# A graph network's first sum takes its first eight source tiles by halves of 256 columns, from block 6 on, then two tiles a block

## What is computed

```
h = relu(layernorm(x)); h = relu(h @ enc_w1.T + enc_b1) @ enc_w2.T + enc_b2
for w in conv_w:                                  # 5 layers
    agg = segment_sum((h @ w)[src], dst)          # sum over a node's edges
    gi, gh = agg @ gru_wih.T + gru_bih, h @ gru_whh.T + gru_bhh
    r = sigmoid(ir + hr); z = sigmoid(iz + hz); n = tanh(i_n + r * h_n)
    h = (1 - z) * n + z * h
x = x + sigmoid(relu(relu(h) @ dec_w1.T + dec_b1) @ dec_w2.T + dec_b2)
h = relu(layernorm(x))
out = x + (A @ relu((A @ h) @ W1.T + b1)) @ W2.T + b2   # A: normalized adjacency
```

## Time and profile before

| | us |
|---|---|
| median of three runs (lowest, highest) | 739.68 (739.09, 739.78) |
| the profiled execution | 739.29 |
| its span | 737.4 |
| PE busy | 720.2 (98%) |
| DVE busy | 331.2 (45%) |
| ACT busy | 316.5 (43%) |

### The profile page before, as it was taken

The page is one execution under the profiler, slowest core; times in us unless marked ns, Lnnn a source line. Parts: engine busy times, 40 slices in busy tenths (PEclk is TensorE's granted clock), DMA queues, the critical chain, the costliest instruction groups (busy, mean ns, idle before and its releaser), DMA issues.

```text
span 737.4 us, 9911 instructions
## 1 busy us (share of the span) xinstructions
PE 720.2 (98%) x4071; PEld 394.2 (53%) x4071; DVE 331.2 (45%) x665; ACT 316.5 (43%) x467; POOL 43.6 (6%) x57
## 2 busy tenths in 40 slices
PE   6989999999999999999999999999999999999998
PEld 4556666445444454444444444444445545558887
DVE  7999997625032241133221223656644632122532
ACT  5978876737244344244452334432447411122000
POOL 4230000000000000000000000120002220000000
DMA  6020000835003232022230212610002000000100
GB/s 168 4 91 10 3 4 3 157 60 90 2 6 64 55 53 39 1 49 44 59 64 0 49 37 38 119 61 2 1 0 93 15 1 1 1 1 3 37 24 32
DMA packets 79240, 28.41 MB, mean 39 GB/s; under 512 B 70519, under 2 KB 78390, under 8 KB 79062
## 3 DMA queue, kind: packets, MB, share of 16 engines
q1 hardware_dynamic: 78230, 26.93, 17.1%
q0 software_dynamic: 240, 0.66, 0.3%
q10 hardware_dynamic: 720, 0.13, 0.1%
HBM read 8.03 MB, written 2.60 MB: 14 GB/s over the span
## 4 chain that ended last, share of the span: by engine, by line
PE 85%; DVE 9%; ACT 2%; DMA 1%; POOL 1%; issue 1%; SPq 0%; ACTq 0%; DVEq 0%; POOLq 0%
PE PSA L1260 35%; PE PSA L1477 9%; PE PSA L1342 7%; PE PSA L1421 5%; PE PSA L1205 4%; PE PSA L1273 4%; PE PSA L1282 4%; PE PSA L1281 3%; PE PSA L1277 3%; PE PSA L1275 3%; PE PSA L1284 3%; DVE CT L877 3%; PE PSA L1409 2%; PE PSA L1397 1%; DVE stat L839 1%; DMA H<-yS 1%
## 5 line engine op out<-in xcount | busy, mean ns | idle before, releaser
L1260 PE MATMUL PSA<-AT,H 128*128 128x512 fp8e3 (+1 forms) x1470 | 275.8, 347 | 0.3 <-DMA H<-yS 0.2
L1260 PEld LDWEIGHTS PSA<-AT,H 128*128 128x128 f16 x1470 | 126.7, 98 | 151.4 <-issue 12.0
L1090 DVE SCALAR_TENSOR_TENSOR rS<-PSA,bias,rS 128x512 f32<-128x512 f32 (+1 forms) x35 | 23.9, 683 | 261.0 <-ACT rS L1660 261.0
L1660 ACT ACTIVATE rS<-PSA,bias 128x512 f32<-128x512 f32 (+1 forms) x35 | 22.1, 632 | 198.9 <-PE PSA L1281 198.9
L1584 ACT ACTIVATE AT<-PSA 128x1000 fp8e3<-128x1000 f32 (+1 forms) x79 | 74.5, 1000 | 18.5 <-PE PSA L1205 17.3
L1558 ACT ACTIVATE CTL<-AT 128x3125 fp8e3<-128x3125 fp8e3 (+1 forms) x25 | 69.9, 2797 | 0.0
L1421 PE MATMUL PSA<-CT,H 128*128 128x512 fp8e3 (+1 forms) x336 | 65.5, 351 | 0.3 <-POOL H L767 0.3
L1477 PE MATMUL PSA<-AT,CT 128*128 128x256 f16 x576 | 65.1, 273 | 0.6 <-DVE AT L1027 0.6
L1477 PEld LDWEIGHTS PSA<-AT,CT 128*128 128x128 fp8e3 x576 | 55.4, 98 | 7.3 <-DVE AT L1027 0.8
L1342 PE MATMUL PSA<-AT,H 128*128 128x512 fp8e3 x245 | 58.0, 379 | 0.0
L877 DVE TENSOR_TENSOR CT<-CT 128x2048 bf16<-128x2048 bf16 x40 | 48.7, 1217 | 0.0
(11 more groups left out here) (186 smaller groups left out, 662.3 us busy)
## 6 DMA issues: line engine op xcount, KB each, us to landing
AT<-scale_scratch SPq DMA_DIRECT2D x1, 1562.5 KB, 6.3
H<-in_x SPq DMA_DIRECT2D x1, 1536.0 KB
out<-AT SPq DMA_DIRECT2D x12, 128.0 KB
comb_scratch<-CT SPq DMA_DIRECT2D x1, 960.0 KB, 4.7
comb<-comb_scratch SPq DMA_DIRECT2D x5, 192.0 KB, 2.9
H<-yS SPq DMA_TRANSPOSE x48, 2.5
H<-in_x SPq DMA_DIRECT2D x1, 512.0 KB
CT<-AT SPq DMA_TRANSPOSE x25, 4.0
```

What stands on the lines that cost most here:

```text
L1260: last = nc.tensor.matmul(bank[:, 0:w], H16[:, l % 2, t, h, :], AT3[:, t, n0:n0 + w], start=(t == 0 and h == 0), stop=(t == T - 1))
```

## The change

A new table HALVES and a function `aggregate_half`: chunk 0's tiles 0 to 7 are summed for its left 256 columns and its right 256 columns apart, 8 matmuls for four tiles of a half. The left half asks for the counts of blocks 0 to 3 only, the right one for those of blocks 0 to 6. The left half of tiles 0 to 3 is in block 6, which had no part of the sum. Tiles 8 to 19, which were spread over blocks 10, 12, 13 and 14 by 4, 2, 2 and 4, go by two into each of the blocks 9 to 14. From block 15 on the table is what it was.

```diff
--- before.py
+++ after.py
@@ -248,9 +248,12 @@
         KEYS_AT = {5: 1, 12: 2, 20: 3, 28: 4}
         ROWS_AT = {7: 2, 11: 3, 15: 4}
         assert all(b + 1 < k * (PW // J) for b, k in KEYS_AT.items())
-        PART = {7: [(0, 0, 4)], 8: [(0, 4, 8)], 10: [(0, 8, 12)], 12: [(0, 12, 14)], 13: [(0, 14, 16)], 14: [(0, 16, 20)],
-                15: [(1, 0, 4)], 16: [(0, 20, 24)], 17: [(1, 4, 8)], 18: [(0, 24, T), (1, 8, 11)]}
-        PART.update({19: [(1, 11, 14)], 20: [(1, 14, 18)], 21: [(1, 18, 21)], 22: [(1, 21, T)]})
+        HALF = TC * P // 2
+        LEFT, RIGHT = slice(0, HALF), slice(HALF, 2 * HALF)
+        HALVES = {6: [(LEFT, 0, 4)], 7: [(RIGHT, 0, 4), (LEFT, 4, 8)], 8: [(RIGHT, 4, 8)]}
+        PART = {9: [(0, 8, 10)], 10: [(0, 10, 12)], 11: [(0, 12, 14)], 12: [(0, 14, 16)], 13: [(0, 16, 18)], 14: [(0, 18, 20)],
+                15: [(1, 0, 4)], 16: [(0, 20, 24)], 17: [(1, 4, 8)], 18: [(0, 24, T), (1, 8, 11)],
+                19: [(1, 11, 14)], 20: [(1, 14, 18)], 21: [(1, 18, 21)], 22: [(1, 21, T)]}
         EVEN = [0, 4, 7, 11, 14, 18, 21, T]
         PART.update({23 + 7 * i + g: [(2 + i, EVEN[g], EVEN[g + 1])] for i in range(2) for g in range(7)})
         PART.update({37 + g: [(4, EVEN[g], EVEN[g + 1])] for g in range(NBT - 37)})
@@ -259,7 +262,7 @@
         assert max(PART) < NBT
         for q in range(AHEAD + 1):
             done = [(t0, t1) for b in sorted(PART) for q1, t0, t1 in PART[b] if q1 == q]
-            assert [t0 for t0, _ in done] == [0] + [t1 for _, t1 in done][:-1] and done[-1][1] == (T if q < AHEAD else BEGUN)
+            assert [t0 for t0, _ in done] == [0 if q else 2 * TC] + [t1 for _, t1 in done][:-1] and done[-1][1] == (T if q < AHEAD else BEGUN)
         EA, EB, EC2 = 6, 1, 7
         agg_bank = lambda q: PS[(0, TB, 1, CB)[q] if q < AHEAD else AGG[q % 2]]
         filled = lambda w: 2 * ((w + J * W - 1) // (J * W))
@@ -1344,6 +1347,17 @@
                 if t1 == T:
                     last.then_inc(sum_ready, 1)
 
+            def aggregate_half(half, t0, t1):
+
+                pe.wait_ge(window_bank_free, filled(half.stop))
+                if half == LEFT and t0 == 0:
+                    pe.wait_ge(comb_copied, L)
+                pe.wait_ge(encoded_lo, t1 // TC)
+                for t in range(t0, t1):
+                    for h in range(2):
+                        nc.tensor.matmul(agg_bank(0)[:, half], H16[:, 0, t, h, :], AT3[:, t, half],
+                                         start=(half == LEFT and t == 0 and h == 0), stop=False)
+
             transposed_keys(0)
             encoder(0)
             for b in range(NBT):
@@ -1354,6 +1368,8 @@
                     encoder(step(b))
                 if b in COMB:
                     combine(COMB.index(b))
+                for half, t0, t1 in HALVES.get(b, []):
+                    aggregate_half(half, t0, t1)
                 for q, t0, t1 in PART.get(b, []):
                     aggregate_part(q, t0, t1)
```

## The result

The changed kernel takes 740.87 us (median of 18 runs, 740.72 to 741.53), the kernel before 739.61 (18 runs, 739.09 to 739.82). The ratio is 1.0019, 95% interval 1.0013 to 1.0026: 1.26 us slower, where 0.15 us faster was forecast, and outside the range (738.7 to 740.7) by 0.17 us. The loss is clear of noise: by the interval it is 1.0 to 1.9 us. The prediction took 1.48 us for the least that can be told, which was too coarse. The profiled execution took 740.84 us with a span of 739.1, which is 1.7 us more than the 737.4 before.

What follows compares the result with a forecast made beforehand. VectorE's one-hot tables were taken to set TensorE's pace up to block 16, which starts 0.15 us earlier. Span 737.4 - 0.15 = 737.25, profiled time 739.14, plus 0.39 for the median: 739.5 us, range 738.7 to 740.7.

Steps and rivals of the forecast that it cites:

- The order and the start of each block: TensorE's blocks 7 to 16: forecast starts, such as block 8 at 41.62, block 15 at 63.40, block 16 at 66.74.
- The price of a half: Each 256-column matmul of the sum takes 0.109 us, so 32 take 3.49 against 3.46 for the 16 full ones.
- The 0.028 us at 53 columns: Price per matmul read from L1260, weight loads included, as evidence that 16-bit weights should not matter to a half.
- The new wait on bank 0's copy in block 6: Block 6's halves wait for ScalarE's copy out of bank 0 and start at 38.03, not at 36.65.
- the lateness of block 7: Block 7's counting, queued behind the halves, starts at 38.90 instead of 37.53, 1.37 us late; the delay is gone by block 9.
- The cap by VectorE's table at block 16: Block 16's table is ready at 66.68, so TensorE gains only 0.15 us there and waits 0.36 for VectorE.
- Rival 2: Weight loads don't hide behind halves: block 16 is 1.27 us late (chance 0.03) or 3.39 late (chance 0.03).
- rival 3: Block 6's halves delay block 7 and the delay stays to the end: 1.37 us, 741.0 us; chance 0.02.
- The rule on weight loads: The skill's rule that a load overlaps a running matmul only across row groups: 107 ns ahead of each half, median 741.2.
- from block 16 on TensorE's list is the same in both kernels: Claim that TensorE's work after block 16 is unchanged, so block 16's start matters most.
- a constant 0.15 us from there to the end: Sign of being right: the gain at block 16 neither grows nor vanishes through the rest of the program.
- code that is laid out otherwise in memory: Leftover case with no place or size given, either faster or slower; chance 0.02.

Runs made afterwards that it cites:

- experiment 8: The new order of tiles by full matmuls, without halves, and VectorE's last row numbers in block 16 instead of 15; 739.45 us against 739.82 for the kernel before.
- experiment 1: The kernel before with 16 unused tiny matmuls (32 instructions) ahead of block 7's counting; 740.92 us against 739.49, ratio 1.0019.
- experiment 6: The kernel before with 64 unused tiny matmuls (128 instructions), half ahead of block 7 and half ahead of block 8; 739.58 us against 739.82.
- experiment 5: The kernel before with 32 unused tiny matmuls (64 instructions) ahead of block 7's counting; 739.08 us against 739.82, ratio 0.9990.

## Why the prediction was wrong

By its steps. The order and the start of each block: right, to 0.1 us in every one. The price of a half, 0.109 us: right. (The 0.028 us at 53 columns came from a row's length, which holds the modelled end of the last matmul; from start to start it is 168.03 to 169.26, 0.025. Nothing hung on it.) The new wait on bank 0's copy in block 6 and the lateness of block 7, 1.37 us (38.94 for 37.53 is 1.41): right, and swallowed by block 9 as reckoned. The cap by VectorE's table at block 16: right, shown by experiment 8, with 0.24 us of wait where 0.36 was forecast. Rival 2 (loads in front of the halves) and rival 3 (the delay stays): didn't happen. The rule on weight loads that the prediction cites from the Trainium skill, "TensorE: Matmul & The Clock Gate", "The mechanism", is contradicted a second time, by the halves themselves: 16 pairs of load and matmul in 1.75 us.

The step that failed is "from block 16 on TensorE's list is the same in both kernels", and with it "a constant 0.15 us from there to the end": its sum put at nothing what the added instructions do far behind the place of the change. The runs showed 1.19 and 0.94 us of wait there, 1.26 us by the medians, and 1.43 from 32 added instructions alone (experiment 1). The list is the same, but it begins 32 instructions later in the program, and its instructions come by transfers that share the DMA engines with the state transposes. I gave "code that is laid out otherwise in memory" 0.02, with no place and no price. The place could be read from the profile before; of the price it held only a sign. The row of the wait for H<-yS, 0.16 us in the kernel before, says that the ends of the layers had no time to spare. The instruction queue stands on the profile's page, and 32 instructions less in front of the next block are some 3.5 us at 0.216 us for two. Laid against the transposes from 175.5 to 179.4, a block at 181.7 that comes 3.2 us earlier falls among them.

What is not shown is why a transfer of 16 KB costs so much. Small packets that are under way hang, for up to 1.0 us at the first layer's end, 1.5 at the fourth's and 1.7 in experiment 6, and chunk 4 lands 1.7 us later (181.01 for 179.31). Whether the queues take turns, or a transpose must drain before it goes on, these runs don't tell.

## What to carry to other kernels

Where an engine runs a long program without loops, count the instructions that a change adds ahead of a tight place, and look where that engine's instruction transfers fall in it: moving them by a few instructions that fit into a wait can cost or give more than the change. When a change of a kernel loses time far behind the place that it touches, first try the old kernel with as many idle instructions more. Look also for the single buffer whose reuse makes such a delay into a chain.

## What was not expected of the hardware

One transfer of 16 KB of instructions that meets chunk 4's transposes cost TensorE 0.7 to 1.2 us, in five kernels and at three of the four ends of layers. The same transfer at chunk 5's transposes cost about 0.3 at each of two ends (the kernel before against experiment 5, by the two timelines), and beside the first transpose of chunk 4 it cost ScalarE 0.18 and TensorE nothing that is seen. The Trainium skill, "Runtime: NRT & Kernel Launch", section "Instruction fetch mechanics", calls the cost of crossing such a block mostly hidden. That fits the others of the 33 in so far as no other wait of TensorE for H<-yS is listed, and fails for these; what each of the others costs was not measured.
